# Softmax and normalisation work moved between the stages of a mixture-of-experts tail

## The reference, cut to what matters

```python
x  = x + layernorm(mamba(layernorm(x)))               # x1
xn = layernorm_affine(layernorm(x))                   # two normalisations in a row
logits   = (xn / |xn| * scale) @ (mu / |mu|)          # rows x 256 slots
dispatch = softmax(logits, axis=rows)                 # a denominator for each column
combine  = softmax(logits, axis=slots)                # a denominator for each row
slot_in  = dispatch.T @ xn                            # 256 x 512
slot_out = gelu(slot_in @ w1 + b1) @ w2 + b2          # per expert
out      = combine @ slot_out
x  = x + layernorm(out)
```

## Time and profile before

| stretch of the span | us | from | to |
|---|---|---|---|
| Mamba stack | 7258 | 0 | 7258 |
| stage 1, `moe_logits` | 379 | 7258 | 7637 |
| stage 2, `moe_dispatch` | 210.5 | 7637 | 7847.5 |
| stage 3, `moe_combine` | 221.2 | 7847.5 | 8068.7 |

### The profile page before, as it was taken

How to read it: one execution, slowest core, us unless ns; L and a number is a source line. 1 busy time by engine, 2 the same in 40 slices (tenths; PEclk the granted TensorE clock), 3 DMA queues, 4 the chain that set the end, 5 groups by cost and what they waited for, 6 DMA issues and landing times. The chain is left out here.

```text
span 8068.7 us, 103428 instructions
## 1 busy us (share of the span) xinstructions
PE 7221.5 (89%) x31688; PEld 4128.2 (51%) x31688; DVE 7450.5 (92%) x8498; ACT 5928.7 (73%) x11165; POOL 6709.5 (83%) x2904
## 2 busy tenths in 40 slices
PE   7899999999999999999999999999999999877886
PEld 3555555555555555555555555555555555446752
DVE  3999999999999999999999999999999999976617
ACT  6787788878877877777777777777777777644415
POOL 4999999999999999999999999999999999962103
PEclk9999999999999999999999999999999999887889
DMA  2111111111121111211111111111111111115424
GB/s 84 59 65 65 66 60 65 58 61 57 61 65 65 65 66 60 66 55 58 63 53 53 54 55 55 54 50 54 54 54 47 53 53 54 49 39 199 188 84 156
DMA packets 230099, 549.39 MB, mean 68 GB/s; under 512 B 27024, under 2 KB 27280, under 8 KB 210768
## 3 DMA queue, kind: packets, MB, share of 16 engines
q1 hardware_dynamic: 196304, 458.25, 18.0%
q10 hardware_dynamic: 33280, 84.95, 2.7%
HBM read 441.39 MB, written 101.71 MB: 67 GB/s over the span
## 5 line engine op out<-in xcount | busy, mean ns | idle before, releaser
L1082 POOL TENSOR_TENSOR bu<-w,b_rep 128x1024 f32<-128x1024 f32 x2048 | 4807.3, 2365 | 541.8 <-DVE h L1162 531.3
L1162 DVE TENSOR_TENSOR_SCAN h<-decay,h_last,bu 128x512 f32<-128x512 f32 x3840 | 4814.1, 1274 | 14.0 <-ACT decay L853 14.0
L585 PEld LDWEIGHTS turn<-ident_m,h 128*128 128x128 f32 x16384 | 1948.2, 142 | 2707.8 <-DVE acc L1182 1325.0
L853 ACT ACTIVATE decay<-delta,neg_a 128x512 f32<-128x512 f32 x4096 | 2777.4, 690 | 648.2 <-DVE h L1162 609.6
L585 PE MATMUL turn<-ident_m,h 128*128 128x128 f32 x16384 | 2556.2, 280 | 425.4 <-DVE acc L1182 351.1
L1182 DVE SCALAR_TENSOR_TENSOR acc<-turn,c_now,acc 128x512 f32<-128x512 f32 x3072 | 2243.7, 730 | 71.9 <-ACT c_now L881 43.2
L869 ACT ACTIVATE prod<-turn,c_now 128x512 f32<-128x512 f32 x1024 | 701.0, 685 | 503.4 <-PE turn L585 367.9
L1097 POOL TENSOR_TENSOR prod<-prod 128x1024 f32<-128x1024 f32 x448 | 1057.8, 2361 | 10.6 <-ACT prod L869 10.6
L511 PE MATMUL proj<-x_conv,w_in 128*128 128x512 f32 x2048 | 1041.6, 600 | 4.2 <-ACT x_conv L843 1.0
L511 PE MATMUL proj<-zy,w_out 128*128 128x512 f32 x2048 | 1009.7, 597 | 24.0 <-ACT u L754 20.5
L511 PE MATMUL proj<-conv_in,conv_diag 128*128 128x512 f32 x2048 | 1024.8, 594 | 0.2 <-ACT halo L746 0.2
(11 more groups left out here) (170 smaller groups left out, 6058.5 us busy)
## 6 DMA issues: line engine op xcount, KB each, us to landing
b_rep<-b_rows SPq DMA_DIRECT2D x1024, 256.0 KB, 3.2
x_gate<-xt SPq DMA_DIRECT2D x32, 1024.0 KB, 7.0
xt<-stage ACTq DMA_DIRECT2D x128, 256.0 KB, 2.4
x_conv<-xt SPq DMA_DIRECT2D x31, 1024.0 KB, 6.9
x_gate<-in_x_dram SPq DMA_DIRECT2D x16, 1024.0 KB, 6.7
x_l<-in_x_dram SPq DMA_DIRECT2D x16, 1024.0 KB, 5.9
mt_l<-xt SPq DMA_DIRECT2D x16, 1024.0 KB, 5.7
x<-x_l ACTq DMA_DIRECT2D x16, 1024.0 KB, 6.3
```

Source lines behind the costliest of these rows:

```text
L585: mm = pe.transpose(out[:, b * P:(b + 1) * P], h[:, (G * GROUPS + k) % H_RING, b, j * P:(j + 1) * P], ident[:])
L853: act.activation(decay[:, (G * SLOTS_BODY + s) % DEC_RING, :], delta[:, blk, :], ACT.Exp, scale=neg_a[:, n, blk:blk + 1]).then_inc(decay_s ...
L1082: pool.tensor_tensor(bu[:, (G * PAIRS + s // 2) % BU_RING, :, :], w[:, blk:blk + 2, :], b_rep[:, g % B_RING, :].unsqueeze(1).to_broadcast( ...
L1162: dve.tensor_tensor_scan(h[:, (G * GROUPS + k) % H_RING, b, :], decay[:, (G * SLOTS_BODY + s) % DEC_RING, :], bu[:, (G * PAIRS + s // 2) % ...
```

## The change

In stage 1 the two roots become one: 1/sqrt(v(1+eps)+eps²) is what the two normalisations come to. In stage 2 the single-column products leave the loop; GpSimd adds the exponentials of all chunks into `e_sum`, and eight products behind the loop sum its partitions. Stage 2 also takes over the row softmax: VectorE finds the row maxima, and ScalarE overwrites the logits with their exponentials and leaves the row sums in `den_c`. In stage 3 the row exponentials are gone, TensorE transposes the stored ones, and the normalisation is written without the division by the row sum: exp(-0.5 ln(variance + eps·den²)). The loops of all three stages are written out for each chunk; `Fori` is gone from them.

```diff
-def pipelined(eng, depth, step, ahead=0):
-    for i in range(depth):
-        step(i, i % 2, [n <= i for n in range(depth + 1)])
-    rest = (NC - depth - ahead) // 2 * 2
-    with eng.Fori(0, rest // 2) as pair:
-        for s in range(2):
-            step(2 * pair + (depth + s), (depth + s) % 2, [True] * (depth + 1))
-    for i in range(depth + rest, NC + depth):
-        step(i, i % 2, [i - n < NC for n in range(depth + 1)])
+def pipelined(eng, depth, step):
+    for i in range(NC + depth):
+        step(i, i % 2, [0 <= i - n < NC for n in range(depth + 1)])
...
 # moe_logits, VectorE
                 dve.wait_ge(sd2_set, c + 1)
-                chain = Chain(dve, r2_step, c * 2)
-                chain.link(dve.reciprocal(r2[:], sd2[:]))
-                chain.link(dve.tensor_tensor(q[:], mv2[:, :, 1], r2[:], ALU.mult))
-                dve.tensor_tensor(q[:], q[:], r2[:], ALU.mult).then_inc(q_set, 1)
-            if live[1]:
-                dve.wait_ge(sd3_set, c + 1)
-                chain = Chain(dve, r3_step, c * 2)
-                chain.link(dve.reciprocal(r3[:], sd3[:]))
-                chain.link(dve.tensor_tensor(r3[:], r3[:], r2[:], ALU.mult))
+                chain = Chain(dve, r3_step, c)
+                chain.link(dve.reciprocal(r3[:], sd2[:]))
...
 # moe_logits, ScalarE
-                act.activation(sd2[:], mv2[:, :, 1], ACT.Sqrt, bias=eps[:]).then_inc(sd2_set, 1)
-            if live[1]:
-                act.wait_ge(q_set, c + 1)
-                act.activation(sd3[:], q[:], ACT.Sqrt, bias=eps[:]).then_inc(sd3_set, 1)
+                act.activation(sd2[:], mv2[:, :, 1], ACT.Sqrt, scale=1.0 + LN_EPS, bias=eps_sq[:]).then_inc(sd2_set, 1)
...
 # moe_dispatch, GpSimd
+        pool.sem_inc(e_added, 2)
+        pool.memset(e_sum[:], 0.0).then_inc(e_added, 1)
+        for pair in range(0, NC // 2):
+            i = 2 * pair
+            for s in range(2):
+                c = i + s
+                pool.wait_ge(e_added, c + 3)
+                pool.wait_ge(e_set, c + 3)
+                pool.tensor_tensor(e_sum[:], e_sum[:], e[:, s], ALU.add).then_inc(e_added, 1)
...
 # moe_dispatch, VectorE, behind diff
+                dve.wait_ge(row_set, c + 1)
+                dve.tensor_reduce(neg_row[:, s], logits[:, bass.ds(c * J, J), :], AX_X, ALU.max, negate=True).then_inc(row_top, 1)
         dve.wait_ge(summed, NC + 2)
+        dve.wait_ge(den_set, 1)
...
 # moe_dispatch, ScalarE
                 act.wait_ge(summed, c + 1)
+                act.wait_ge(e_added, c + 2)
                 act.activation(e[:, s], diff[:, s], ACT.Exp).then_inc(e_set, 1)
+                act.wait_ge(row_top, c + 1)
+                for j in range(J):
+                    row = logits[:, bass.ds(c * J + j, 1), :].rearrange("p a s -> p (a s)")
+                    ins = act.activation(row, row, ACT.Exp, bias=neg_row[:, s, j:j + 1], accum_out=den_c[:, bass.ds(c * J + j, 1)])
+                ins.then_inc(row_set, 1)
...
 # moe_dispatch, TensorE
-                        pe.matmul(sums[:, h, :], e[:, s, j, h * P:(h + 1) * P], xh[:, s, j, :], start=False, stop=False, skip_group_check=True)
-                        mm = pe.matmul(den[:, h, 0:1], e[:, s, j, h * P:(h + 1) * P], ones[:], start=False, stop=False, skip_group_check=True)
+                        mm = pe.matmul(sums[:, h, :], e[:, s, j, h * P:(h + 1) * P], xh[:, s, j, :], start=False, stop=False, skip_group_check=True)
                 mm.then_inc(summed, 1)
+        pe.wait_ge(e_added, NC + 3)
+        for h in range(2):
+            for j in range(J):
+                mm = pe.matmul(den[:, h, 0:1], e_sum[:, j, h * P:(h + 1) * P], ones[:], start=j == 0, stop=j == J - 1)
+        mm.then_inc(den_set, 1)
...
 # moe_combine, VectorE; tops() and its calls are gone
-            chain.link(dve.reciprocal(rden[:, js], den[:, bass.ds(c * J + hf * H, H)]))
-            chain.link(dve.tensor_tensor(var[:, js], mv[:, js, 1], rden[:, js], ALU.mult))
-            dve.tensor_tensor(var[:, js], var[:, js], rden[:, js], ALU.mult).then_inc(var_set, 1)
+            sums = den[:, bass.ds(c * J + hf * H, H)]
+            chain.link(dve.scalar_tensor_tensor(var[:, js], sums, LN_EPS, sums, ALU.mult, ALU.mult))
+            dve.tensor_tensor(var[:, js], var[:, js], mv[:, js, 1], ALU.add).then_inc(var_set, 1)
...
-            chain.link(dve.reciprocal(mul[:, js], sd[:, js]))
-            chain.link(dve.tensor_tensor(mul[:, js], mul[:, js], rden[:, js], ALU.mult))
...
 # moe_combine, ScalarE; the exponentials of a step are gone
+        act.preload_act_table_set("natural_log_exp_and_others")
...
-            act.activation(sd[:, js], var[:, js], ACT.Sqrt, bias=eps[:]).then_inc(sd_set, 1)
+            act.activation(log[:, js], var[:, js], ACT.Ln).then_inc(log_step[hf], 1)
+            act.wait_ge(log_step[hf], c + 1)
+            act.activation(mul[:, js], log[:, js], ACT.Exp, scale=-0.5).then_inc(mul_set, 1)
...
 # moe_combine, TensorE
-                pe.wait_ge(e_set, i + 3)
                 pe.wait_ge(et_set, i + 2)
```

More of the change, by code:

```diff
@@ L1323, in _ @@
         pool.memset(eps[:], LN_EPS)
+        pool.memset(eps_sq[:], LN_EPS * LN_EPS)
         pool.memset(ones[:], 1.0).then_inc(const_set, 1)
@@ L1468, in step @@
                 ins.then_inc(rn_set, 1)
-            if live[0] and not (isinstance(i, int) and i == NC - 1):
+            if live[0] and i < NC - 1:
                 norm_of_x(i + 1, 1 - s)
@@ L1483, in step @@
                 act.activation(xsq[:], xnt[:, s1], ACT.Square).then_inc(xsq_set, 1)
-        pipelined(act, 2, step, ahead=1)
+        pipelined(act, 2, step)
         for s in range(2):
@@ L1594, in _ @@
             sp.dma_start(b2[p0:p0 + per, e8 // half, :], d["b2"][e8].partition_broadcast(per)).then_inc(w_in, 16)
-        with sp.Fori(1, NC // 2) as pair:
+        for pair in range(1, NC // 2):
             i = 2 * pair
@@ L1616, in _ @@
         dve.sem_inc(diff_set, 2)
-        with dve.Fori(0, NC // 2) as pair:
+        for pair in range(0, NC // 2):
             i = 2 * pair
@@ L1642, in _ @@
         act.sem_inc(e_set, 2)
-        with act.Fori(0, NC // 2) as pair:
+        act.sem_inc(row_set, 2)
+        for pair in range(0, NC // 2):
             i = 2 * pair
@@ L1675, in _ @@
                 pe.matmul(sums[:, h, k * P:(k + 1) * P], zeros[:], ident[:], start=False, stop=False, skip_group_check=True)
-            pe.matmul(den[:, h, 0:1], zeros[:], ones[:], start=True, stop=False, skip_group_check=True)
-        with pe.Fori(0, NC // 2) as pair:
+        for pair in range(0, NC // 2):
             i = 2 * pair
@@ L1703, in _, with moe_combine @@
         mm.then_inc(out_ps, 1)
-def moe_combine(nc, ctx, d, logits, slot_out):
+def moe_combine(nc, ctx, d, e, slot_out, den):
     sb, ps, sem = makers(nc, ctx, "_c")
@@ L1743, in _ @@
     def _(pool):
-        pool.memset(eps[:], LN_EPS).then_inc(eps_set, 1)
         build_identity(pool, ident, ident_set)
         pool.sem_inc(sum_set, 2)
-        with pool.Fori(0, NC // 2) as pair:
+        for pair in range(0, NC // 2):
             i = 2 * pair
@@ L1761, in _ @@
             sp.dma_start(x1[:, s], d["x1"][s]).then_inc(x1_in[s], 16)
-        with sp.Fori(0, NC // 2 - 1) as pair:
+        for pair in range(0, NC // 2 - 1):
             i = 2 * pair
@@ L1807, in step @@
                 variance(i - 2, 0)
-                coefficients(i - 2, 0)
+                bias(i - 2, 0)
                 variance(i - 2, 1)
-            if live[0] and not (isinstance(i, int) and i == NC - 1):
-                tops(i + 1, 1 - s)
             if live[2]:
-                coefficients(i - 2, 1)
+                bias(i - 2, 1)
             if live[0]:
@@ L1818, in step @@
                 dve.tensor_copy(et[:, s], turn[:]).then_inc(et_set, 1)
-        pipelined(dve, 2, step, ahead=1)
+        pipelined(dve, 2, step)
     @block.scalar
     def _(act):
-        act.sem_inc(e_set, 2)
         act.sem_inc(y_set, 2)
-        act.wait_ge(eps_set, 1)
+        act.preload_act_table_set("natural_log_exp_and_others")
         def norm(c, s1, hf):
@@ L1838, in step @@
         def step(i, s, live):
-            if live[0]:
-                act.wait_ge(top_set, i + 3)
-                act.wait_ge(turned, i + 1)
-                for j in range(J):
-                    ins = act.activation(e[:, s, j, :], logits[:, bass.ds(i * J + j, 1), :].rearrange("p a s -> p (a s)"),
-                                         ACT.Exp, bias=neg_top[:, s, j:j + 1], accum_out=den[:, bass.ds(i * J + j, 1)])
-                ins.then_inc(e_set, 1)
             if live[2]:
@@ L1897, in build @@
         slot_out = whole.enter_context(nc.sbuf_tensor("slot_out", [P, 2, D_MODEL], F32))
+        den_c = whole.enter_context(nc.sbuf_tensor("den_c", [P, NC * J], F32))
         with ExitStack() as ctx:
```

60 lines of the change are left out of this document (25 added, 35 removed).

## The result

The changed kernel takes 7988.88 us (median of 4 runs, 7986.42 to 7990.49) against 8072.39 us before in the same session (4 runs, 8067.1 to 8074.62): a ratio of 0.9897, 95% interval 0.988 to 0.9914. The forecast was 7983, range 7970 to 8003. Since the range covers three of the rivals too, the stages have to say whether it was right for its reasons.

What follows compares the result with a forecast made beforehand. No engine is full in any stage; chunk-to-chunk chains bound stages 1 and 3, TensorE stage 2's loop. Gains 14.2 + 22.9 + 53.1 = 90.2 us off 8070.5, plus 2.9 to the median, give 7983 us, range 7970 to 8003.

Steps and rivals of the forecast that it cites:

- The 0.88 us: Stage 1: with one root, the normalisation can begin 0.88 us earlier per step, and this passes along the chain.
- rival (c): Stage 1 gains nothing because TensorE at its lower clock ends the chain: 7997 us; chance 0.05.
- ScalarE's 3.1 us a chunk: Stage 2: ScalarE's added exponentials, 3.1 us per chunk, lie beside TensorE's 6.88 us and cost nothing.
- The ring: Stage 3: the chain from one GpSimd addition to the next, forecast at 4.71 us a half, 9.42 a chunk.
- the held operation: Stage 3: VectorE's scalar_tensor_tensor is blocked until GpSimd's addition ends; free, a half would be 0.20 us shorter.
- The start: Stage 3: earlier first transposes save 4.2 us, a row maximum and two half rings in the first chunk 1.9.
- the end: Stage 3: the last four halves save 4 x (5.05 - 4.71) = 1.4 us.
- (a): Stage 3: small operations no cheaper or the copy shows, so a half stays at 5.05 us: 7994 us; chance 0.15.
- (b): Stage 3: the scalar_tensor_tensor isn't held by GpSimd, 6 us less: 7977 us; chance 0.08.
- (d): Stage 2: delayed transfers take the place of the removed products: about 8007 us; chance 0.05.
- (e): All stages: the moved work sits on each chain and gives back what it saves: 8073 us; chance 0.02.
- (f): Written-out code must be fetched; at 6 us for each of 16 instruction packets, slower, 8079 us; chance 0.03.

Runs made afterwards that it cites:

- e1: The kernel before with only stage 1's second small root replaced by one root for both normalisations; 8063.47 us.
- e2: The changed kernel with its loops put back as engine loops, except VectorE's in stage 2 and TensorE's in stage 3; 7990.94 us.
- e3: The changed kernel with stage 2's single-column products back in TensorE's loop and GpSimd's running sum gone; 8009.55 us.
- e6: The changed kernel with a square root and reciprocal in place of Ln and Exp in stage 3; 7990.77 us.
- e9: The changed kernel with the expert weights fetched in 1 MB pieces behind the chunks' rows from chunk 2 on; 7972.51 us.
- e10: The changed kernel with eps*den^2 worked out once and given to stage 3's Ln as bias, without VectorE's product and sum per half; 7961.67 us.
- e8: The changed kernel with four unread 128x256 products put among stage 1's 32 single-column products; 7985.24 us.

## Why the prediction was right, and where its terms were off

**Stage 1, 14.2 forecast, 9.8 in the trace.** The 0.88 us passed to the chain: with `ta` slow in both, e1's steps are 0.87 and 0.89 us shorter than those of before. Written-out code adds 0.13 to 0.30 us, so that like for like a step went from 21.34 to 20.34 us where `ta` was slow, and from 20.61 to 19.63 where it was fast. Two things that I had not weighed went against each other. The first is the clock: before, part of the steps had fast transposes; in the changed kernel's trace nearly none has, which costs 0.7 us a step. In the form in which I put rival (c), that TensorE ends the chain by its norms, it was wrong; the low clock entered through `ta`, and took part of the gain, not all. Why the clock falls ahead of `ta` in every step now is not shown. The second is the loops, costed at nothing: e1 and e2 have stage 1 at 374.3 and 373.6 us, the changed kernel and five others with the same written-out code and order of it (e3, e6, e9, e10, and with fillers e8) at 366.8 to 370.3. The 9.8 of the changed kernel's own profile is thus the low end; 380.1 less the 366.8 to 367.7 of e3, e6, e9 and e10 is 12.4 to 13.3. That the sum came near 14.2 is partly luck: some 6 us from the root and 3 to 7 from a term that I had at zero.

**Stage 2, 22.9 forecast, 21.8 measured.** The terms are as put: 0.43 us a product, next to nothing for chunks 0 and 1, 1.84 us behind the loop. What is missing lies behind the loop, where TensorE is slower than before by 1.8 us: the eight transposes of the slot inputs take 1.97 us for 1.10, and the last 32 matmuls 16.60 for 15.71. The granted clock is 0.50 from 7762 to 7765, where it was 1.00 in the same transposes before. Ahead of the loop's end some 0.6 us more were gained than forecast. The transposes, before and changed:

```profile
7796.73 1.10 PE L1691 MATMUL turn_d<-ident_d,slot_in_d 128*128 128x128 f32 x8 [1.71 <-DVE slot_in_d L1627]
```

```profile
7762.68 1.97 PE L1700 MATMUL turn_d<-ident_d,slot_in_d 128*128 128x128 f32 x8 [1.78 <-DVE slot_in_d L1625]
```

e3 gives 21.4 back for the one edit. That ScalarE's 3.1 us a chunk, VectorE's and GpSimd's additions are covered is shown by the products without a gap, though VectorE and GpSimd held each other. The Trainium skill (SBUF — State Buffer, Who interferes with whom) says that whoever issues first has the shared ports and the other blocks fully; the trace agrees, GpSimd's additions taking 3.33 us where the subtraction started 0.11 ahead (7671.14 and 7671.25) and 2.35 where there was none beside.

**Stage 3, 53.1 forecast, 49.1 measured.** The ring, its order and the held operation are right. e10 shows by removal that the hold closes it: the edit also took two small operations away, but the hold is the larger part of what it gave. Off was a size: 4.71 us a half against 4.78 and 4.91. Ln and Exp take 0.203 each, with the hand-over 0.23, where I took 0.19 from a root without a bias. The longer half adds 0.13, which e2 ties to the written-out code. From chunk 0's store to chunk 13's the gain is 41.3 and not 45.6: 3.5 us for the longer halves, and 0.8 because I took 12.93 us for all thirteen intervals of before, where the last was 12.12. The start gave 7.2 for the 6.1 forecast, the end 0.6 for 1.4.

**The rivals.** (a) had the half at 5.05: it is at 4.84 on average, 0.13 of the 0.34 us between that and my 4.71. (b) is wrong, the operation is held. (d) and (e) are wrong by e3. (f) is wrong as put: the instruction packets went from 241 to 254, and in e2 the loops bring no time back on the whole; what written-out code costs is the 1.6 us of stage 3. The three stages together gave 4.4 + 1.1 + 4.0 = 9.5 us less than forecast. Of that 0.7 came back ahead of the stages, and 2.9 is the step from profiled execution to median that the forecast added and the changed kernel did not show (7989.04 profiled, 7988.88 the median). The rest is the forecast's error, 5.9 us.

## What to carry to other kernels

Find what GpSimd holds before moving VectorE's work: the same addition cost nothing beside stage 2's subtractions, 25 us as the link ahead of a logarithm, and 33 us when an order that looked shorter put four tiles beside it. Give ScalarE the sum as a bias, or leave the small operand in PSUM. And before crediting a gain to an edit, compare stages among kernels that share their code: here stage 1 differed by up to 3.5 us among kernels with equal code there.
